# Rope attention with one 64-row score product a head: parts of queries and keys laid out by DMAs, bias rows padded to 128

## What is computed

```python
q = (layernorm(x) @ Wq).reshape(256, 32, 16)        # 32 heads of 16
k, v = split(ctx @ Wkv)                             # ctx is 256 x 256
q, k = rope(q, pos), rope(k, pos)                   # pairs of elements turned by an angle
logits = einsum('qhd,khd->hqk', q, k) / 4
attn = einsum('hqk,khd->qhd', softmax(logits), v)
x = x + tanh(g) * (attn.reshape(256, 512) @ Wout + bout)
```

## Time and profile before

| | us |
|---|---|
| median of 3 runs | 2327.05 (2326.88 to 2328.17) |
| profiled execution, span | 2292.1 |
| of it, rope attention from its first PE transpose to the last output product | 61.8 to 626.9 |
| PE busy in the span | 2046.7 |
| DVE, ACT, POOL busy in the span | 1380.2, 1145.9, 792.6 |

### The profile page before, as it was taken

The page is one execution under the profiler, slowest core; times in us unless marked ns, Lnnn a source line. Parts: engine busy times, 40 slices in busy tenths (PEclk is TensorE's granted clock), DMA queues, the critical chain, the costliest instruction groups (busy, mean ns, idle before and its releaser), DMA issues. The chain is left out here.

```text
span 2292.1 us, 37833 instructions
## 1 busy us (share of the span) xinstructions
PE 2046.7 (89%) x12201; PEld 1479.9 (65%) x12201; DVE 1380.2 (60%) x2748; ACT 1145.9 (50%) x2846; POOL 792.6 (35%) x834
## 2 busy tenths in 40 slices
PE   4699999999869989999999999967899999874993
PEld 1466666665469989999999999943555555522441
DVE  5567767676457745666676666637676767562114
ACT  3477777776433324555555555523565666432110
POOL 1222222221102522444444444426544443135541
PEclk9999999999879999999999999978999999877996
DMA  8311011111042256899888888840111110063446
GB/s 298 87 20 25 15 25 17 23 20 20 1 141 47 29 154 196 238 271 278 245 234 232 248 244 233 227 112 24 24 24 24 26 32 20 10 186 92 138 137 253
DMA packets 165772, 267.62 MB, mean 117 GB/s; under 512 B 42490, under 2 KB 97026, under 8 KB 164356
## 3 DMA queue, kind: packets, MB, share of 16 engines
q1 hardware_dynamic: 130604, 195.20, 28.7%
q0 software_dynamic: 34976, 70.00, 13.4%
HBM read 186.42 MB, written 61.93 MB: 108 GB/s over the span
## 5 line engine op out<-in xcount | busy, mean ns | idle before, releaser
L614 ACT ACTIVATE a_P<-a_SC,a_nm 128x256 f32<-128x256 f32 x512 | 235.9, 473 | 134.4 <-DVE a_nm L519 133.6
L1090 POOL DMA_INDIRECT b_y_rows<-b_ysb,b_entry x94 | 176.0, 1872 | 348.2 <-ACT b_ysb L1233 315.8
L519 DVE TENSOR_REDUCE a_nm<-a_SC 128x2 f32<-128x512 f32 x256 | 164.8, 686 | 144.0 <-PE a_SC L760 144.0
L1302 DVE TENSOR_TENSOR b_wl<-b_raw,b_wh 128x1472 fp32r<-128x1472 f32 x147 | 243.3, 1682 | 4.4 <-ACT b_wh L1225 4.4
L1225 ACT ACTIVATE b_wh<-b_raw 128x1472 fp32r<-128x1472 f32 x147 | 205.2, 1435 | 1.6 <-DMA b_raw<-in_L_ffn_sd 1.6
L1922 ACT ACTIVATE c_P<-c_SC,c_nm 128x240 f32<-128x240 f32 x256 | 115.7, 457 | 101.3 <-DVE c_P L1814 101.3
L1243 ACT ACTIVATE b_ah<-b_AT 128x384 fp32r<-128x384 f32 x126 | 62.0, 492 | 205.9 <-PE b_AT L1155 205.9
L771 PEld LDWEIGHTS a_T<-ident,a_P 128*128 128x128 f32 x1024 | 118.7, 144 | 69.4 <-issue 38.9
L771 PE MATMUL a_T<-ident,a_P 128*128 128x128 f32 x1024 | 145.7, 281 | 17.2 <-DVE a_PT L531 16.1
L1314 DVE TENSOR_TENSOR b_al<-b_AT,b_ah 128x384 fp32r<-128x384 f32 x126 | 70.2, 557 | 145.8 <-ACT b_ah L1243 142.8
L1308 DVE TENSOR_TENSOR b_xl<-b_XT,b_xh 128x512 fp32r<-128x512 f32 x126 | 86.8, 689 | 92.2 <-ACT b_xh L1238 90.8
(11 more groups left out here) (469 smaller groups left out, 5092.8 us busy)
## 6 DMA issues: line engine op xcount, KB each, us to landing
b_raw<-in_L_ffn_wg SPq DMA_DIRECT2D x47, 704.0 KB
b_raw<-in_L_ffn_wu SPq DMA_DIRECT2D x47, 704.0 KB
b_raw<-in_L_ffn_wd SPq DMA_DIRECT2D x47, 512.0 KB
b_raw<-in_L_ffn_wd SPq DMA_DIRECT2D x47, 192.0 KB
table<-st_wide SPq DMA_DIRECT2D x4, 2048.0 KB, 13.9
a_qS<-a_qT SPq DMA_DIRECT2D x128, 64.0 KB, 2.3
c_qS<-c_qT SPq DMA_DIRECT2D x64, 128.0 KB, 2.3
d_M<-table SPq DMA_DIRECT2D x4, 2048.0 KB, 11.1
```

The source lines that it names most:

```text
L519: eng.tensor_reduce(nm[:, g % 4, j, :], SC[j][:, :].rearrange("p (t k) -> p t k", t=BT), AX.X, ALU.max, negate=True).then_inc(topped, 1)
L614: e = eng.activation(Pr[:, i, t, :], SC[j][:, t * S:(t + 1) * S], ACT.Exp, bias=nm[:, g % 4, j, t:t + 1], accum_out=den[:, h, t:t + 1])
L1090: eng.indirect_dma_start(out=y_rows, out_offset=bass.IndirectOffsetOnAxis(ap=entry[:, r % ENT, h, 1:2].bitcast(U32), axis=0), in_=ysb[:, v ...
L1302: eng.tensor_tensor(wl[s % 2][:, cols], raw[s % 2][:, cols], r32(wh[s % 2][:, cols]), ALU.subtract).then_inc(w_lo, 1)
```

## The change

- `scores` makes one product of 64 rows a head and token tile in place of two of 32. Its operands are `q4` and `k4`. A head has 64 rows in each: in `k4` its 32 rows (high, low) twice, in `q4` high, low, and then low, high. `q4` and `k4` are 128 x 16 pairs x 256; head j of the pair stands on partitions 64 j to 64 j + 63.
- `spread_out` takes the place of `exchange`. It lays both out from `qT` and `kT`: 12 DMAs for the queries of a half (4 of 32 partitions, 8 of 16) and 8 for the keys (32 partitions). Each partition gets 4 pieces of 1 KB. The keys' DMAs stand in SP's stream at k1a and k1b. It waits for the scores of the batch before that read the same half (`until_scored`).
- `qT` and `kT` become half as large: both halves of a batch pass through the same place, so the copies to them (`unit`) now wait until the DMAs of the half before have landed (`until_copied`), where they waited for scores.
- `scores` waits, at the first pair of a half, for the semaphores of both kinds of DMAs in place of the four copies and the exchange.
- `ones` and `bias` are 128 rows, with zeros set by two POOL instructions at the block's start, and the bias product has 128 rows.

```diff
-                for n in ("q0" + i, "q1" + i, "k0" + i, "k1" + i):
-                    is_freed(eng, (b, n))
-                eng.wait_ge(swapped["ab".index(i)], 16 * (P // HD) * (b + 1))
+                for n in "qk":
+                    until_copied(eng, n, 2 * b + p // HALF + 1)
...
-                    for half, q in enumerate((qT, qS)):
-                        for j in range(2):
-                            r = R * (2 * (p % 2) + j)
-                            m = eng.matmul(SC[j][:, t * S:(t + 1) * S], q[r:r + R, p // 2, t * P:(t + 1) * P],
-                                           kT[r:r + R, p // 2, :], start=(half == 0), stop=(half == 1))
+                    for j in range(2):
+                        rows = slice(2 * R * j, 2 * R * (j + 1))
+                        m = eng.matmul(SC[j][:, t * S:(t + 1) * S], q4[rows, p, t * P:(t + 1) * P], k4[rows, p, :],
+                                       start=True, stop=True)
...
+                until_scored(eng, b, i)
+                dst, src = (q4, qT) if n == "q" else (k4, kT)
+                for j in range(4):
+                    pairs = slice(HALF * i + j // 2, HALF * (i + 1), 2)
+                    at, of = 2 * R * (j % 2), R * j
+                    moves = [(at, of, R)]
+                    moves += [(at + R, of, R)] if n == "k" else [(at + R, of + HD, HD), (at + R + HD, of, HD)]
+                    for to, fr, k in moves:
+                        eng.dma_start(r32(dst[to:to + k, pairs, :]), r32(src[fr:fr + k, :, :])).then_inc(copied[n], 16)
...
-                until_scored(eng, b, "ab".index(n[-1]))
+                until_copied(eng, n, 2 * b + "ab".index(n[-1]))
```

More of the change, by code:

```diff
@@ L308, in rope_attention @@
     COLUMN_AT = {3: 0, 7: 1, 11: 2, 15: 3}
+    COPIES = {"q": 12, "k": 8}
     def pieces(s):
@@ L340, in rope_attention @@
         lnsc, llw = sb("lnsc", [P, NT, 2]), sb("llw", [P, 5, NT])
-        brow, blow, bias = sb("brow", [1, D]), sb("blow", [1, D], F32R), sb("bias", [2, D], F32R)
-        one, ones = sb("one", [2, P]), sb("ones", [2, P], F32R)
+        brow, blow, bias = sb("brow", [1, D]), sb("blow", [1, D], F32R), sb("bias", [P, D], F32R)
+        one, ones = sb("one", [2, P]), sb("ones", [P, P], F32R)
         ctxb = sb("ctx", [P, BT, CD])
@@ L347, in rope_attention @@
         hlq, hlk = sb("hlq", [P, 2, H, 2, HD]), sb("hlk", [P, 2, H, 2, HD])
-        qT, qS, kT = [sb(n, [P, QUADS, S], F32R) for n in ("qT", "qS", "kT")]
+        qT, kT = [sb(n, [P, QUADS // 2, S], F32R) for n in ("qT", "kT")]
+        q4, k4 = [sb(n, [P, PAIRS, S], F32R) for n in ("q4", "k4")]
         V = [sb(f"V{i}", [P, BT, PAIRS * VW]) for i in range(2)]
@@ L370, in rope_attention @@
         topped, exp_done = sem("topped"), [sem(f"exp_done{j}") for j in range(2)]
-        rec_done, swapped = sem("rec_done"), [sem(f"swapped{i}") for i in range(2)]
+        rec_done, copied = sem("rec_done"), {n: sem(f"copied_{n}") for n in "qk"}
         turned, pt_done = [sem(f"turned{j}") for j in range(2)], [sem(f"pt_done{j}") for j in range(2)]
@@ L405, in unit_target, with until_copied @@
         def unit_target(n):
-            t, i = int(n[1]), "ab".index(n[-1])
+            t = int(n[1])
             dst = qT if n[0] == "q" else kT
-            return dst[:, QUADS // 2 * i:QUADS // 2 * (i + 1), t * P:(t + 1) * P]
+            return dst[:, :, t * P:(t + 1) * P]
+        def until_copied(eng, n, k):
+            ge(eng, copied[n[0]], 16 * COPIES[n[0]] * k)
         def part(n, i):
@@ L433, in context, with spread_out @@
                     eng.dma_start(ctxb[:, t, :], ctx_d[b, t * P:(t + 1) * P, :]).then_inc(ctx_loaded, 16)
-            def exchange(b, i):
+            def spread_out(b, n, i):
                 for t in range(BT):
[L437 to L441, removed]
+                    is_freed(eng, (b, f"{n}{t}" + "ab"[i]))
+                until_scored(eng, b, i)
[7 more added lines that the diff above has]
+                        eng.dma_start(r32(dst[to:to + k, pairs, :]), r32(src[fr:fr + k, :, :])).then_inc(copied[n], 16)
             load_positions(eng)
@@ L455, in _ @@
                 for b, n in items(s):
-                    if n[0:2] == "q1":
-                        exchange(b, "ab".index(n[-1]))
+                    if n[0:2] in ("q1", "k1"):
+                        spread_out(b, n[0], "ab".index(n[-1]))
         @block.gpsimd
@@ L461, in _ @@
             eng.memset(one[:, :], 1.0).then_inc(consts, 1)
+            eng.memset(r32(ones[:, :]), 0.0).then_inc(consts, 1)
+            eng.memset(r32(bias[:, :]), 0.0).then_inc(consts, 1)
             for i in range(2):
@@ L508, in _ @@
             tables(eng)
-            eng.wait_ge(consts, 1)
-            eng.tensor_copy(ones[:, :], one[:, :]).then_inc(bias_set, 1)
+            eng.wait_ge(consts, 3)
+            eng.tensor_copy(ones[0:2, :], one[:, :]).then_inc(bias_set, 1)
             eng.wait_ge(row_in, 16)
@@ L664, in _ @@
             sines(eng)
-            eng.wait_ge(consts, 3)
+            eng.wait_ge(consts, 5)
             for s in range(FIRST, LAST):
@@ L749, in scores @@
                 if p % HALF == 0:
-                    i = "ab"[p // HALF]
-                    for n in ("q0" + i, "q1" + i, "k0" + i, "k1" + i):
-                        is_freed(eng, (b, n))
-                    eng.wait_ge(swapped["ab".index(i)], 16 * (P // HD) * (b + 1))
+                    for n in "qk":
+                        until_copied(eng, n, 2 * b + p // HALF + 1)
                 for j in range(2):
@@ L756, in scores @@
                 for t in range(BT):
-                    for half, q in enumerate((qT, qS)):
-                        for j in range(2):
-                            r = R * (2 * (p % 2) + j)
-                            m = eng.matmul(SC[j][:, t * S:(t + 1) * S], q[r:r + R, p // 2, t * P:(t + 1) * P],
-                                           kT[r:r + R, p // 2, :], start=(half == 0), stop=(half == 1))
-                            if t == BT - 1 and half == 1:
-                                m.then_inc(scored[j], 1)
+                    for j in range(2):
+                        rows = slice(2 * R * j, 2 * R * (j + 1))
+                        m = eng.matmul(SC[j][:, t * S:(t + 1) * S], q4[rows, p, t * P:(t + 1) * P], k4[rows, p, :],
+                                       start=True, stop=True)
+                        if t == BT - 1:
+                            m.then_inc(scored[j], 1)
             def turn_exponentials(g):
```

## The result

| | us |
|---|---|
| median, changed kernel, 4 runs | 2347.24 (2346.10 to 2348.98) |
| median, kernel before, 4 runs beside it | 2326.97 (2321.66 to 2328.17) |
| ratio | 1.0085, 95% interval 1.0068 to 1.0102 |
| profiled execution of the changed kernel, span | 2347.3 |

The change makes the kernel 20 us slower, and the time lies outside the range of the forecast, 2308 to 2341. The first attention, from its first PE transpose to the start of its last bias product, took 564.7 us before and takes 579.2 now: 14.5 of the 20.

The account below looks back on a forecast made before the run. PE's stream, and a ring of scores, maxima and exponentials, were taken to bound the attention. Gains of 31.2 and 4.5 us, less 25.4 of waits and 8 for the clock, left 2.3: forecast 2324.5 us, range 2308 to 2341.

Parts of the forecast that it names:

- gain, scores and bias: Attention: 31.2 us from fewer score products and 4.5 us from bias products on 128 rows.
- waits, batch 0: PE ahead of batch 0's first scores: they come 14.35 us after the first issue, 6.87 before; loss 7.5 us.
- waits, batches 1 to 7: PE ahead of the first scores: DMAs late by 3.85 us in batch 1 and 2.35 in each of six others.
- clock behind them: PE's clock falls behind waits: 2 us for batch 1, four of six others at 1.5; 8 us, bounds 0 to 21.
- What bounds: Attention: PE's stream sets most steps; otherwise a ring of scores, maxima, exponentials, 3.54 us a pair, with neither DVE nor ACT full.
- the two groups for four: Score products on PE: dropping two of a pair's four groups saves 0.24 us a pair, 30.7 us over 128 pairs.
- the bias: Bias product after the output projection on PE: 128 rows for 2 saves 0.28 us, 16 times, 4.5 us.
- DVE waits for the scores even in its fullest steps: DVE in the attention: it waits 0.33 us even in two full steps a batch; only 1 us taken off the gain.
- The other waits were covered: Attention: waits for the queries' DMAs and for half b have enough steps ahead of them, so they cost nothing.
- 35 us outside the span: Whole kernel: 35 us lie outside the profiled span, added to 2289.8 to give 2324.7.
- The late keys: Rival: keys' DMAs, issued last in 1 KB pieces, come later; 2339 to 2350 at the upper bound, 2333 halfway; chance 0.30.
- the scores aren't what bounds: Rival: DVE keeps part of the 31 us; five us less gives 2329.5; counted within the forecast's range, no chance of its own.

Follow-up runs that it names:

- e1: Changed kernel with 8 of each half's 20 DMAs, the rows left out set to zero once, so the output differs; 2300.64 us, ratio 0.9854.
- e4: Changed kernel with the keys' 8 DMAs of each half issued by POOL in place of SP; 2328.7 us, ratio 0.9992.
- e3: Kernel before with twelve more DMAs behind each eight, from scratch to scratch, that nobody waits for; 2330.3 us, ratio 0.9997.
- e8: Changed kernel without the padding of the bias (ones and bias of 2 rows, no fills); 2350.9 us, ratio 1.0079.
- e11: Changed kernel with q1a and k1a one step earlier, and batch 0's half a DMAs shared by SP and ACT; 2308.81 us, ratio 0.9904.

## Why the prediction was wrong, step by step

The terms in us, predicted and measured, for the attention only. The gain is what e1's pairs are shorter, 31.3, and 1.6 that e1 gained behind the last scores. The waits are by how much the step ahead of a batch's first scores is longer than in e1, and the clock by how much the three steps behind them are. Batch 0 is the time from the first issue to the first scores, 15.02 for 6.87:

| | predicted | measured |
|---|---|---|
| gain, scores and bias | 35.7 | 32.9 |
| waits, batch 0 | 7.5 | 8.2 |
| waits, batches 1 to 7 | 17.95 | 26.4 |
| clock behind them | 8 | 12.8 |
| net | +2.3 | -14.5 |

- **What bounds, the two groups for four, the bias: right.** A step between PE's transposes fell from 3.54 to 3.31 and from 3.85 to 3.61; the bias gave 0.28 to 0.34.
- **"DVE waits for the scores even in its fullest steps": wrong for two steps a batch**, and it is where the gain is short. I had looked at steps of one kind. Timeline of DVE, in the second profile of the kernel before, from the maxima of one pair to those of the next:

```profile
249.94 1.29 DVE L519 TENSOR_REDUCE a_nm<-a_SC 128x2 f32<-128x512 f32 x2 [2.27 <-PE a_SC L760]
...
252.90 0.42 DVE L567 TENSOR_TENSOR a_aT<-a_O,a_recT 128x256 f32<-128x256 f32 x1 [0.99 <-ACT a_recT L627]
...
253.84 1.28 DVE L519 TENSOR_REDUCE a_nm<-a_SC 128x2 f32<-128x512 f32 x2
```

  The second maxima have no idle time before them, so DVE doesn't wait for scores there. It isn't full either: it stood idle for 0.99 of these 3.90 us, until ACT had copied the turned reciprocals of the denominators (`recT`), which ACT does behind the four exponentials of the pair. So this step is a chain: maxima, exponentials, `recT`, the product with it, the low part of the keys, the next maxima. The scores don't stand in it. There are two such steps a batch, and in the changed kernel they still take 3.90:

```profile
259.08 1.29 DVE L532 TENSOR_REDUCE a_nm<-a_SC 128x2 f32<-128x512 f32 x2 [1.85 <-PE a_SC L770]
...
262.05 0.42 DVE L580 TENSOR_TENSOR a_aT<-a_O,a_recT 128x256 f32<-128x256 f32 x1 [1.00 <-ACT a_recT L640]
...
262.99 1.28 DVE L532 TENSOR_REDUCE a_nm<-a_SC 128x2 f32<-128x512 f32 x2
```

  2 x 0.24 x 8 = 3.8 us, where I had taken off 1.

- **The waits: the mechanism right, the size too small.** This is the step that failed: 25.4 us of new waits predicted, 34.6 measured. I let the twentieth issue begin 11.9 after the first and the scores 14.35 after it. The twentieth began 12.3 to 13.5 after (12.7 in batch 3), and the scores came 14.9 to 16.1 after. The term that I had put at nothing, by taking the count times a clean pitch, is the slow single issue: in six of eight batches one took 0.3 to 1.2 longer than the rest. Timeline of SP, batch 2:

```profile
213.70 8.80 SPq L452 DMA_DIRECT2D a_q<-a_qT  x12
222.66 5.11 SPq L452 DMA_DIRECT2D a_k<-a_kT  x8
```

  8.80 for the twelve that took 7.67 in batch 3, because the ninth took 1.74 us. Batch 1 had no slow issue, and its scores came 14.9 after the first, so the rest is some 0.5 us a batch: a pitch of 0.64 for 0.63; 0.7 to 0.8, and not 0.63, from the twelfth issue to the thirteenth; and 2.55 to 2.7, once 3.56, from the last issue to the scores, for 2.46. By my own rate each 0.1 us costs 0.8 over the eight batches. The trace of the kernel before held the slow issues too; I had read the pitch from two clean trains. The view of the tile `a_qS` there gives the least, the median and the greatest length of an issue, in ns:

```profile
L441 SPq DMA_DIRECT2D a_qS<-a_qT x128: 507/590/1725, 85.6 to 549.6; - x128
```

  Three of these 128, with pieces of 4 KB, took over 0.85 us, and ten of the 320 in the changed kernel, with pieces of 1 KB. What makes an issue slow stays open.

- **The clock: too kind.** I took four falls of six, at 1.5 each, and 2 for batch 1. There were six of six, at 1.5 to 2.5 each, and 1.4 for batch 1. The waits were longer than I had them (3.3 to 4.1, for 2.35), and the clock stayed low for 3.4 us or more. In batches 2 to 7 of e4, where the waits were about as long as I had taken (1.7 to 2.8), it fell with four of six, which is my count, but at 1.7 us three times and 3.1 once.
- **The order of events for batch 0: right.** PE waited there for the keys, and all of it was new loss.
- **The other waits were covered, and traffic was small beside the engines: right** (e3). Inside a train of DMAs it isn't small, 0.76 of the DMA engines over 88 to 98 us; no run shows that this makes the changed kernel's DMAs late.
- **"35 us outside the span": wrong.** The profiled execution of before was shorter in its feed-forward stage, 899.6 us against 931 to 938 in all other profiles; in the second profile of before the time is 1.7 us over the span. It did no harm, since the forecast was a difference, but a sum made against a span should name this gap as unexplained, and not as time outside the kernel.
- **The rivals.** The late keys it was, in the place and at the upper bound that I gave that rival, 2339 to 2350. Its reason, the pieces of 1 KB, isn't shown: the pitch and the landing grew by only 0.02 and some 0.1 us, and slow issues come with pieces of 4 KB as well. I gave it 0.30, and ended the range at 2341, in the middle of it. Of the rival that the scores aren't what bounds a part is true, the two steps a batch above.
- **Left open:** 14.5 us of the 20.3 are in the attention. The last two stages, which the change doesn't touch, took 486.6 and 279.4 in the profile of the changed kernel, and 483.0 and 273.5 in the second one of before. Over all kernels here they vary from 481 to 487 and from 272 to 286, with no order that I can see. No run tells whether these 6 us belong to the change. With the attention's terms right the forecast would have been 2341.5, at the end of the range; the rest of the way to 2347.2 is in this open part.

## What to carry to other kernels

When a change adds DMAs ahead of a consumer, write down the whole chain from the first issue to the consumer (count x pitch, the gap between groups, the landing, and a hiccup or two) and compare it with the distance in the schedule; here some 15.5 us met a distance of 12, and one step earlier in the order was worth 37 us, more than the 33 that the change gains. Read the longest issue of the trace, not only the usual one. Then ask for the margin, not for equality: a wait of 1.8 us in a stream that was otherwise full was paid a second time through the clock. And read the waiting engine's idle time in every step of a batch, not in one, before you let a gain stand in all of them.

## What was not expected of the hardware

- **Idle times of PE that are nearly alike kept the clock and lost it, and a shorter one lost it where a longer one kept it.** In e4 an idle time of 2.71 kept the clock and one of 1.81 lost it; in e8 idle times of 3.21 and 3.27 kept it, and in the changed kernel 3.22 lost it. The scores behind them, on PE's timeline:

```profile
226.16 0.50 PE L773 MATMUL a_SC<-a_k,a_q 64*128 64x256 f32 x4 [2.71 <-DMA a_q<-a_qT]
...
288.88 0.50 PE L773 MATMUL a_SC<-a_k,a_q 64*128 64x256 f32 x4 [1.81 <-DMA a_q<-a_qT]
```

  and the windows to the next scores:

```profile
226.16:229.77 3.61, 3.61 (x20) 2.30 (x20) 3.07 (x6) 3.34 (x11) 0.86 (x2) 1.00 0.00 0
288.88:294.18 5.30, 5.30 (x21) 2.91 (x21) 3.15 (x6) 3.35 (x11) 2.08 (x2) 0.68 0.15 32
```

  and from e8, batch 6, the scores and the window to the next:

```profile
497.58 0.51 PE L768 MATMUL a_SC<-a_k,a_q 64*128 64x256 f32 x4 [3.21 <-issue]
...
497.58:501.20 3.62, 3.62 (x22) 2.31 (x22) 3.11 (x6) 2.27 (x9) 0.91 (x2) 1.00 0.00 0
```

  What decides between them no run shows.

- **SP's issues took longer while POOL issued too.** SP's twelve took 7.7 us alone and 11.8 beside POOL's eight, which kept a pitch of 0.56 to 0.58. Whether POOL's issues or the data in flight slowed them isn't shown; the issues that SP and ACT shared in e11, with the DMA engines full, stayed at 0.59 to 0.86 each.
- **An issue's price depended on what it copies, and hardly on its pieces.** From HBM two issues took 0.41 each; between two places in SBUF each took 0.60 and began 0.64 after the last with pieces of 1 KB, and 0.59 and 0.62 with pieces of 4 KB.
- **The DMA engines, for copies inside SBUF in pieces of 1 KB, were full at 216 to 233 GB/s** (share 1.01 to 1.15, in e11).
